# Decay exponents in four row tiles, and a step-size chain on 128 partitions

## What is computed

```python
dt = jax.nn.softplus(dt + dt_bias)            # step sizes: 256 positions x 8 heads
A = -jnp.exp(A_log)
dA = jnp.einsum('bclh,h->bhcl', dtc, A)
ss = cs[..., :, None] - cs[..., None, :]      # cs = cumsum(dA), one row per head
Lmat = jnp.exp(where(tril, ss, -inf))         # 256 x 256 for each head
Y_diag = jnp.einsum('bcln,bcsn,bhcls,bcshp->bclhp', Cc, Bc, Lmat, xdt)
```

## Time and profile before

| | |
|---|---|
| median of 3 runs | 3832.78 us (3832.23 to 3832.92) |
| the profiled execution | 3836.82 us, its span 3835.1 us |
| TensorE matmul busy | 3601.6 us, 94% |
| VectorE busy | 2728.9 us, 71% |
| ScalarE busy | 1797.4 us, 47% |
| GpSimd busy | 1843.6 us, 48% |
| DMA | 301.54 MB, mean 79 GB/s |
| granted TensorE clock, mean | 0.987 of full |

### The profile page before, as it was taken

The page is one execution under the profiler, slowest core; times in us unless marked ns, Lnnn a source line. Parts: engine busy times, 40 slices in busy tenths (PEclk is TensorE's granted clock), DMA queues, the critical chain, the costliest instruction groups (busy, mean ns, idle before and its releaser), DMA issues. The chain is left out here.

```text
span 3835.1 us, 68187 instructions
## 1 busy us (share of the span) xinstructions
PE 3601.6 (94%) x20666; PEld 2974.8 (78%) x20666; DVE 2728.9 (71%) x8412; ACT 1797.4 (47%) x3656; POOL 1843.6 (48%) x2019
## 2 busy tenths in 40 slices
PE   5999999999999999999999999989879999999998
PEld 4777777777777777777777777777668888888887
DVE  3888888888888888888888888878634444444444
ACT  2555555555555555555555555555422233223322
POOL 3445445444544454444445444544444455445443
PEclk8999999999999999999999999999989999999999
DMA  3111111111111111111111111111045555555554
GB/s 96 33 33 36 47 33 33 37 46 33 36 38 41 33 36 47 33 33 36 46 33 36 38 41 33 36 34 46 17 150 195 192 192 197 189 199 191 197 189 136
DMA packets 148541, 301.54 MB, mean 79 GB/s; under 512 B 20192, under 2 KB 120800, under 8 KB 130336
## 3 DMA queue, kind: packets, MB, share of 16 engines
q0 software_dynamic: 38272, 196.40, 15.0%
q1 hardware_dynamic: 75424, 71.23, 5.9%
q10 hardware_dynamic: 34816, 33.56, 2.8%
HBM read 248.48 MB, written 52.65 MB: 79 GB/s over the span
## 5 line engine op out<-in xcount | busy, mean ns | idle before, releaser
L1003 PE MATMUL bank<-xn1T,w_in 128*128 128x256 f32 (+1 forms) x2560 | 605.5, 387 | 46.0 <-DVE conv L736 45.3
L674 ACT ACTIVATE decay<-bank,w_up 128x256 f32<-128x256 f32 x568 | 269.4, 474 | 700.4 <-PE bank L1204 692.7
L1003 PEld LDWEIGHTS bank<-xn1T,w_in 128*128 128x128 f32 (+1 forms) x2560 | 440.5, 180 | 186.3 <-issue 119.4
L1204 PE MATMUL bank<-zs,w_up 128*128 128x256 f32 x2272 | 504.8, 380 | 0.6 <-ACT zs L540 0.6
L1218 PE MATMUL bank<-w_dn,decay 128*128 128x256 f32 x2272 | 502.1, 379 | 0.0
L736 DVE SCALAR_TENSOR_TENSOR conv<-bank,conv_w,conv 128x255 f32<-128x255 f32 (+2 forms) x960 | 460.1, 479 | 32.9
L1204 PEld LDWEIGHTS bank<-zs,w_up 128*128 128x128 f32 x2272 | 433.6, 191 | 60.4 <-issue 0.9
L1218 PEld LDWEIGHTS bank<-w_dn,decay 128*128 128x128 f32 x2272 | 426.2, 190 | 55.1
L1009 PE MATMUL bank<-w_rel,hT 128*128 128x256 f32 x2048 | 466.4, 381 | 0.7 <-ACT hT L540 0.7
L952 DVE TENSOR_TENSOR hT<-bank,w_dn 128x256 f32<-128x256 f32 x142 | 60.3, 425 | 539.2 <-PE bank L1218 539.2
L420 POOL TENSOR_SCALAR masks<-adjt_sb 128x512 fp32r<-128x512 int32 x256 | 429.1, 1692 | 5.4
(11 more groups left out here) (212 smaller groups left out, 6910.4 us busy)
## 6 DMA issues: line engine op xcount, KB each, us to landing
token_rows<-row SPq DMA_DIRECT2D x64, 260.0 KB
adj_sb<-in_adj SPq DMA_DIRECT2D x64, 256.0 KB
x_sb<-in_x ACTq DMA_DIRECT2D x64, 256.0 KB, 2.8
xT_sb<-in_xT ACTq DMA_DIRECT2D x64, 256.0 KB, 3.0
adjt_sb<-in_adjT SPq DMA_DIRECT2D x64, 256.0 KB
out<-row SPq DMA_DIRECT2D x64, 256.0 KB, 2.2
w_in<-token_rows,idc POOLq DMA_INDIRECT x142
out<-hT,ids POOLq DMA_INDIRECT x142
```

Of the source, the lines that this page charges most:

```text
L674: nc.scalar.activation(hid(f), bank[f % 4][:, 0:GROUP], ACT.Relu, bias=b1[q % 2][:, f:f + 1]).then_inc(hid_ready, 1)
L1003: ins = mm(dst, w_in[:, k, first:first + width], xn1T[:, k, :], start=k == 0, stop=k == DK - 1)
L1204: ins = mm(bank[f % 4][:, 0:GROUP], w1[i][:, k, f * P:(f + 1) * P], xgT[:, k, :], start=k == 0, stop=k == DK - 1)
```

## The change

Per head group of four, `expo` now issues its work in another order and shape. First it writes the mask of each of the four heads with one matmul of 2 x 128 columns, which also opens the accumulation; the waits for the banks stand here. Then come the `sel` products of all four heads, first the 256-column ones, then the 128-column ones, and then the `selneg` products in the same order. Each of these contracts over 24 partitions that lie in one block of 32: head q of the group uses partitions 32q to 32q+23 and its own bank. The last four release `expo_made`. Of 48 matmuls a graph, 8 go: 8 masks and 32 tiled ones are left.

So that each block of 32 partitions has the three parts of all eight heads, the step sizes' weights are laid out 16 times in host memory (`dt_w`), the projection gives 128 partitions in place of 8, and the whole chain runs on 128 partitions. The splitting is done by factors for each partition: `less_hi` and `less_mid` are 0 or -1. It has four instructions in place of five.

`sel` and `selneg` have two slots in place of eight and are built by VectorE from an iota; on GpSimd their two memsets, that of `cs3` and six `affine_select`s go. One load of 128 KB is added, and two small ones grow from 8 to 128 values.

```diff
-        sel = sb("sel", [72, H, P], BF16)
-        selneg = sb("selneg", [72, H, N], BF16)
+        sel = sb("sel", [P, H // 4, P], BF16)
+        selneg = sb("selneg", [P, H // 4, N], BF16)
...
+            (w_dt, by_tile(io["dt_w"])),
...
-            gp.memset(cs3[:], 0.0)
-            gp.memset(sel[:], 0.0)
-            gp.memset(selneg[:], 0.0)
-            for i, part in enumerate((0, 32, 64)):
...
+            gp.iota(row_no[:], [[0, 1]], base=0, channel_multiplier=1)
...
-                    v = bank[2][0:H, N:2 * N]
+                    v = bank[2][:, N:2 * N]
...
+            dve.wait_ge(built, 2)
+            v.tensor_scalar(row_head[:], row_no[:], H - 1, None, ALU.bitwise_and)
...
+            for u in range(H // 4):
+                v.tensor_scalar(sel[:, u, :], ones_row[:, 0:P], mine[:, u:u + 1], None, ALU.mult)
+                v.tensor_scalar(selneg[:, u, :], ones_row[:], mine_neg[:, u:u + 1], None, ALU.mult)
...
-                    ch2.link(dve, v.tensor_tensor_scan(cs[:], ones_row[0:H, :], dA[:], 0.0, ALU.mult, ALU.add), b2_)
+                    ch2.link(dve, v.tensor_tensor_scan(cs[:], ones_row[:], dA[:], 0.0, ALU.mult, ALU.add), b2_)
+                    ch2.link(dve, v.tensor_copy(cs_h[:], cs[:]), b2_)
+                    ch2.link(dve, v.scalar_tensor_tensor(cs_r[:], cs_h[:], less_hi[:], cs[:], ALU.mult, ALU.add), b2_)
+                    ch2.link(dve, v.tensor_copy(cs_m[:], cs_r[:]), b2_)
                     need(dve, expo_made, 8 * b2_)
-                    ch2.link(dve, v.tensor_copy(cs3[0:H, :], cs[:]), b2_)
-                    ch2.link(dve, v.tensor_tensor(cs_r[:], cs[:], cs3[0:H, :], ALU.subtract), b2_)
-                    v.tensor_copy(cs3[32:32 + H, :], cs_r[:])
-                    ch2.link(dve, v.tensor_copy(cs_m[:], cs_r[:]), b2_)
-                    v.tensor_tensor(cs3[64:64 + H, :], cs_r[:], cs_m[:], ALU.subtract).then_inc(cs_ready, 1)
+                    v.scalar_tensor_tensor(cs3[:], cs_m[:], less_mid[:], cs_r[:], ALU.mult,
+                                           ALU.add).then_inc(cs_ready, 1)
...
-                    o = bank[EXPO[h % 4]]
-                    for first, width, s, l in ((0, N, 0, 0), (N, TRI - N, P, P)):
-                        mm(o[:, first:first + width], sel[:, h, :], cs3[:, l:N], start=True, stop=False)
-                        mm(o[:, first:first + P], identb[:], negmask[:], start=False, stop=False,
-                           skip_group_check=True)
-                        ins = mm(o[:, first:first + width], cs3[:, s:s + P], selneg[:, h, 0:width], start=False,
-                                 stop=True)
-                    ins.then_inc(expo_made, 1)
+                    mm(bank[EXPO[h % 4]][:, :].rearrange("p (s l) -> p s l", s=T)[:, :, 0:P], identb[:],
+                       negmask[:].unsqueeze(1).broadcast_to([P, T, P]), start=True, stop=True)
+                for first, width, s, l in ((0, N, 0, 0), (N, TRI - N, P, P)):
+                    for h in heads:
+                        q, u = h % 4, h // 4
+                        mm(bank[EXPO[q]][:, first:first + width], sel[32 * q:32 * q + 3 * H, u, :],
+                           cs3[32 * q:32 * q + 3 * H, l:N], start=False, stop=False, skip_group_check=True)
+                for first, width, s, l in ((0, N, 0, 0), (N, TRI - N, P, P)):
+                    for h in heads:
+                        q, u = h % 4, h // 4
+                        ins = mm(bank[EXPO[q]][:, first:first + width], cs3[32 * q:32 * q + 3 * H, s:s + P],
+                                 selneg[32 * q:32 * q + 3 * H, u, 0:width], start=False, stop=True,
+                                 skip_group_check=True)
+                        if s:
+                            ins.then_inc(expo_made, 1)
...
-                    project(bank[2][0:H, N:2 * N], 2 * DIN + 2 * NS, H).then_inc(proj_made, 1)
+                    for k in range(DK):
+                        ins = mm(bank[2][:, N:2 * N], w_dt[:, k, :], xn1T[:, k, :], start=k == 0, stop=k == DK - 1)
+                    ins.then_inc(proj_made, 1)
...
+    given["dt_w"] = np.ascontiguousarray(np.tile(given["L0_ffn_W_in"][:, -P // copies:], (1, copies)))
```

More of the change, by code:

```diff
@@ L104, in graph_mamba_moe @@
         negmask = sb("negmask", [P, P], BF16)
-        sel = sb("sel", [72, H, P], BF16)
-        selneg = sb("selneg", [72, H, N], BF16)
+        sel = sb("sel", [P, H // 4, P], BF16)
+        selneg = sb("selneg", [P, H // 4, N], BF16)
+        row_no = sb("row_no", [P, 1], I32)
+        row_head, row_quad, row_part = (sb(n_, [P, 1], I32) for n_ in ("row_head", "row_quad", "row_part"))
+        head_off = sb("head_off", [P, 1])
+        mine, mine_neg = sb("mine", [P, H // 4]), sb("mine_neg", [P, H // 4])
+        less_hi, less_mid = sb("less_hi", [P, 1]), sb("less_mid", [P, 1])
         ones_row = sb("ones_row", [P, N])
@@ L115, in graph_mamba_moe @@
         w_in = sb("w_in", [P, DK, 2 * DIN + 2 * NS + H])
+        w_dt = sb("w_dt", [P, DK, P])
         conv_w = sb("conv_w", [P, CB, TAPS])
         conv_b = sb("conv_b", [P, CB])
-        dt_b = sb("dt_b", [H, 1])
-        a_log = sb("a_log", [H, 1])
-        a_neg = sb("a_neg", [H, 2])
+        dt_b = sb("dt_b", [P, 1])
+        a_log = sb("a_log", [P, 1])
+        a_neg = sb("a_neg", [P, 2])
         d_col = sb("d_col", [P, XB])
@@ L161, in graph_mamba_moe @@
         bT, cT = sb("bT", [NS, N]), sb("cT", [NS, N])
[L162 to L165, removed]
+        dt_abs, dt_exp, dt_ln = sb("dt_abs", [P, N]), sb("dt_exp", [P, N]), sb("dt_ln", [P, N])
+        dt_pos, dt, dA, cs = sb("dt_pos", [P, N]), sb("dt", [P, N]), sb("dA", [P, N]), sb("cs", [P, N])
+        cs3 = sb("cs3", [P, N], BF16)
+        cs_h, cs_r, cs_m = sb("cs_h", [P, N], BF16), sb("cs_r", [P, N]), sb("cs_m", [P, N], BF16)
         xdt = pair("xdt", F32, DIN)
@@ L226, in graph_mamba_moe @@
         cpos, cneg, czero = sb("cpos", [P, D]), sb("cneg", [P, D]), sb("czero", [P, D])
-        loads, built, built_v, prep_pe, prep_v, prep_a = map(
-            sem, ("loads", "built", "built_v", "prep_pe", "prep_v", "prep_a"))
+        loads, built, rows_named, built_v, prep_pe, prep_v, prep_a = map(
+            sem, ("loads", "built", "rows_named", "built_v", "prep_pe", "prep_v", "prep_a"))
         x_in, adj_in, adjt_in = map(sem, ("x_in", "adj_in", "adjt_in"))
@@ L281, in graph_mamba_moe @@
             (w_in, by_tile(io["L0_ffn_W_in"])),
+            (w_dt, by_tile(io["dt_w"])),
             (conv_w, by_tile(io["L0_ffn_conv_w"])),
             (conv_b, io["L0_ffn_conv_b"].rearrange("(c p) -> p c", p=P)),
-            (dt_b, col(io["L0_ffn_dt_bias"])),
-            (a_log, col(io["L0_ffn_A_log"])),
+            (dt_b, col(io["dt_bias"])),
+            (a_log, col(io["A_log"])),
             (norm_w, io["L0_ffn_norm_w"].rearrange("(c p) -> p c", p=P)),
@@ L684, in _ @@
             v = nc.vector
+            dve.wait_ge(built, 2)
+            v.tensor_scalar(row_head[:], row_no[:], H - 1, None, ALU.bitwise_and)
+            v.tensor_scalar(row_quad[:], row_no[:], 5, None, ALU.logical_shift_right)
+            v.tensor_scalar(row_part[:], row_no[:], 3, 3, ALU.logical_shift_right,
+                            ALU.bitwise_and).then_inc(rows_named, 1)
+            dve.wait_ge(rows_named, 1)
+            v.tensor_tensor(head_off[:], row_head[:], row_quad[:], ALU.subtract)
+            v.tensor_scalar(less_hi[:], row_part[:], 1.0, -1.0, ALU.is_ge, ALU.mult)
+            v.tensor_scalar(less_mid[:], row_part[:], 2.0, -1.0, ALU.is_ge, ALU.mult).then_inc(rows_named, 1)
+            dve.wait_ge(rows_named, 2)
+            for u in range(H // 4):
+                v.tensor_scalar(mine[:, u:u + 1], head_off[:], 4.0 * u, None, ALU.is_equal)
+                ins = v.tensor_scalar(mine_neg[:, u:u + 1], head_off[:], 4.0 * u, -1.0, ALU.is_equal, ALU.mult)
+            ins.then_inc(rows_named, 1)
+            dve.wait_ge(rows_named, 3)
+            carry(dve)
+            for u in range(H // 4):
+                v.tensor_scalar(sel[:, u, :], ones_row[:, 0:P], mine[:, u:u + 1], None, ALU.mult)
+                v.tensor_scalar(selneg[:, u, :], ones_row[:], mine_neg[:, u:u + 1], None, ALU.mult)
             dve.wait_ge(loads, 16 * len(small))
-            dve.wait_ge(built, 5)
             dve.wait_ge(w_sum_made, 1)
@@ L974, in _ @@
             mm, turn = nc.tensor.matmul, nc.tensor.transpose
-            pe.wait_ge(built, 5)
+            pe.wait_ge(built, 2)
             pe.wait_ge(loads, 16 * len(small))
@@ L999, in turn_pair, with project @@
                 return ins
-            def project(dst, first, width=P):
+            def project(dst, first):
                 for k in range(DK):
-                    ins = mm(dst, w_in[:, k, first:first + width], xn1T[:, k, :], start=k == 0, stop=k == DK - 1)
+                    ins = mm(dst, w_in[:, k, first:first + P], xn1T[:, k, :], start=k == 0, stop=k == DK - 1)
                 return ins
@@ L1247 @@
```

(4 more changed lines are left out.)

12 lines of the change are left out of this document (3 added, 9 removed).

## The result

The changed kernel takes 3858.55 us (3855.95 to 3858.97, 4 runs) against 3832.68 us before (4 runs). The ratio is 1.0066, 95% interval 1.0049 to 1.0084: slower by 0.7% and clear of noise, where 3806 us had been forecast, and outside the range. The profiled execution took 3858.97 us, its span is 3857.2 us.

The account below looks back on a forecast made before the run. Bound: a 42.17 us round alternating between VectorE (22.96) and TensorE (19.2). Gain 0.74 less 0.29 a round over 62 rounds, 27.9 us, plus 1, less 2 at the start: 3806 us, range 3780 to 3838 (own range to 3824).

Parts of the forecast that it names:

- the part on the second group: Exponents of heads 4 to 7, behind `relate(1)` beside VectorE's work: TensorE's saved 0.74 us gains nothing; loss 0.29 us a round.
- the sum: Whole kernel: 27.9 us gained in 62 rounds, 1 us in two outer rounds, 2 us lost once; -27 us.
- The cycle: One round of 42.17 us, set by VectorE and TensorE in turn, with handovers at the relational sum and first taps.
- VectorE's part: From the relational sum through residual, norms, gating and routing to the first taps: 22.96 us of the round.
- TensorE's part: From the first taps until `relate(1)` has ended, with the first four heads' `expo` inside: 19.2 us of the round.
- the first group's gain: First four heads' `expo`, ahead of `relate(1)`: `relate(1)` starts earlier, gain 0.74 us a round.
- The group's time: Four heads' `expo` on TensorE: masks 0.44, tiled matmuls 0.43, two shape changes of 0.10; 1.07 us in place of 1.81.
- the cover for `xdt`: Masks of the first four heads: `xdt` ends about 1508.0, before TensorE needs it; without this, 0.2 us lost.
- The late release: Exponents of heads 4 to 7 start only when all four are nearly done; VectorE's fourth pair 0.29 us late.
- The forecast of 0.45: Net gain per round in us: 0.74 from the first four heads less 0.29 from the other four.
- The serial rival: Tiled matmuls run one after another, 1.34 us a group: +78 us, 3911; chance 0.16, shared with mostly serial or later exponent releases.
- The start: Loads queued on SyncE before the rounds: one more, two with more descriptors; +2 us once, ends 0 and 5.

Follow-up runs that it names:

- the filling: Changed kernel plus 16 matmuls of 128 columns, result unread, where TensorE idles ahead of the normalised transposes: 3789.98 us, ratio 0.9881 to the kernel before.
- The version with a full second group: Changed kernel with heads 4 to 7 issued as before, as full-array matmuls head after head, first four heads still tiled: 3786.79 us, ratio 0.9869 to the kernel before.

## Why the prediction was wrong

**The step that failed** stands in the part on the second group: "TensorE, which frees itself 0.74 us sooner in this group, gains nothing with that". A gain of nothing was right; a cost of nothing was not. It rests on an earlier sentence, that the change "can win TensorE time but no clock" because the clock is at the upper level already. That row also says what there is to lose, and neither the sum nor a rival had this term. It measures 1.12 us a round (42.55 against 41.43 with the filling), 63 distances of it 71 us. The Trainium skill has the rule that I left out: "TensorE: Matmul & The Clock Gate", Part 1, says that the throttled level is the default and that activity releases it. The trace agrees, since work that nobody uses brings the clock back from 0.94 to 1.00.

**The cycle** was named rightly. VectorE's part and TensorE's part meet where they were said to; the first group's gain comes through to the round (44 us for the first alone), and the second's doesn't: rounds without a fall take 42.20 us with the second group tiled alone and 42.12 with neither. In the filled run, where the clock stays up, VectorE's part is 1553.02 - 1529.99 = 23.03 us, where it was 22.96, and TensorE's is 1571.44 - 1553.02 = 18.42, where it was 19.2.

```profile
1529.99 0.69 DVE L829 TENSOR_TENSOR row<-bank,x2b 128x512 f32<-128x512 f32 x1 [0.68 <-PE bank L1025]
1553.02 1.34 PE L1019 MATMUL bank<-xn1T,w_in 128*128 128x256 f32 x5 [1.05 <-DVE conv L752]
1571.44 0.69 DVE L829 TENSOR_TENSOR row<-bank,x2b 128x512 f32<-128x512 f32 x1 [0.68 <-PE bank L1025]
```

**The group's time** was 1.07 us in the forecast and is 0.97: masks up to the first tile 1523.16 - 1522.63 = 0.53 us with the change of shape, as 0.44 + 0.10 had it, and the tiles 0.44 up to the start of `relate(1)`, where 0.43 + 0.10 stood. The change back shows one matmul later: the 16 of `relate(1)` take 3.72 us, where they took 3.67. The drain that the Trainium skill announces for a change of the tiling mode ("TensorEngine Tiling (Array Packing)", Key Properties) is 0.09 us one way and 0.05 the other by this, below the 0.16 worked out for it. The 3.07 times of the Trainium skill ("TensorE: Matmul & The Clock Gate", Measured speedup vs the span model; an estimate of 0.44 us) fits the 0.44 of the trace, but so do 16 issues of 0.027 us; the runs don't tell the two apart. So the first group gains 1.81 - 0.97 - 0.05 = 0.79, not 0.74; VectorE's wait for it went from 1.83 to 0.7, and the cover for `xdt` held.

**The late release** was mis-sized: 0.29 us in the forecast, 0.06 in the trace. From the relational sum to the attention's residual VectorE takes 1531.51 - 1527.53 = 3.98 us, where it took 3.92. The forecast took 0.45 us as ScalarE's own distance between two exponentials, from rows in which ScalarE was waiting for TensorE's next head: 1.81 / 4 is 0.45 as well. Released together, four last 1.64 us, (1.64 - 0.49) / 3 = 0.38 apart, and most of the delay is made up. VectorE in the changed kernel:

```profile
1527.53 0.69 DVE L829 TENSOR_TENSOR row<-bank,x2b 128x512 f32<-128x512 f32 x1 [0.68 <-PE bank L1025]
1529.57 1.83 DVE L760 TENSOR_TENSOR decay<-decay,g 128x768 f32<-128x768 f32 x2
1531.51 0.88 DVE L843 SCALAR_TENSOR_TENSOR x<-bank,rsum,x_sb 128x256 f32<-128x256 f32 x2
```

Together these give 0.79 - 0.06 = 0.73 us a round without the clock, and 42.17 - 0.73 = 41.44 is what the filled version takes (41.43). The version with a full second group, which has no late release there, takes 41.39. The forecast of 0.45 was too careful about everything it had thought of, and the sign came from what it had not.

**The serial rival** did not happen in the changed kernel, and in no order of the tiled matmuls. **The start** gained 1.9 us where 2 were to be lost; the loads were not the burden that I made of them.

## What to carry to other kernels

Where TensorE isn't the only bound, work taken from it beside another engine's critical stretch turns into one long idle stretch; look up how much idle time stands there already and what comes next, because the matmuls behind it may run at half the clock, as the projection's did here. Tile or shorten only the group on the path, and leave the hidden one as it is. If a kernel gets slower with less work, compare the granted clock window by window before anything else, and test it with filling matmuls.

## What the chip showed

Behind idle time of 1.05 us, followed by another 0.44, TensorE's clock fell in nearly every round of the changed kernel, at a cost of 0.50 or 1.88 us a fall; with 0.23 us of filling it stayed up in most. Behind 1.02 to 1.06 us other versions had it fall in 22 to 51 of some 52 rounds, so the length alone doesn't decide.

Four row tiles of 24 rows, with a bank each, ran 16 matmuls (3072 columns in sum) in 0.44 us, and it made hardly a difference whether neighbours in the program used different tiles or the same (0.97 and 1.00 us a group), though 16 of 256 columns in a single tile and bank take 0.116 us each. How the engine brings that about, these traces don't show.

A change from the full array to row tiles cost 0.09 us here, the change back 0.05, which shows between the first two matmuls behind it (0.32 us apart in place of 0.27).

A pace read from the trace can belong to the engine ahead: ScalarE's exponentials were 0.45 us apart while TensorE released them one by one, and are 0.38 apart when all four are ready.
